# One convolution pair in every slot, begun in slot 10 of the image two ahead, with rounding 12 pairs ahead

## What is computed

```python
# layer 0: quantised 3x3 convolution
v = _gn(x)                                   # 8 groups of 2 channels, per image
scale_input = max(abs(v)) / 128              # over ALL images
x_q = round(clip(v / scale_input, -127, 127))
x = x + conv3x3(x_q, weight_int8) * (scale_input * scale_weight) + bias
# layer 1: 3x3 convolution in the frequency domain
X = rfftn(_gn(x), axes=(-2, -1))
Yr = conv(Xr, wr) - conv(Xi, wi) + b_real
Yi = conv(Xr, wi) + conv(Xi, wr) + b_imag
x = x + irfftn(Yr + 1j * Yi)
```

## Time and profile before

| what | us |
|---|---|
| median of 3 executions (lowest, highest) | 3791.02 (3787.89, 3796.55) |
| the profiled execution | 3767.42 |
| its span, first to last instruction | 3765.6 |
| first pass and set-up, to the first halo copy | 597.2 |
| statistics of slot 10 (L855), first and last of the 32 | 674.8 and 3671.6 |

### The profile page before, as it was taken

The page is one execution under the profiler, slowest core; times in us unless marked ns, Lnnn a source line. Parts: engine busy times, 40 slices in busy tenths (PEclk is TensorE's granted clock), DMA queues, the critical chain, the costliest instruction groups (busy, mean ns, idle before and its releaser), DMA issues.

```text
span 3765.6 us, 126495 instructions
## 1 busy us (share of the span) xinstructions
PE 2979.5 (79%) x45732; PEld 2646.9 (70%) x45732; DVE 3117.7 (83%) x5880; ACT 1893.1 (50%) x2799; POOL 1490.4 (40%) x1984
## 2 busy tenths in 40 slices
PE   0000004899999999999999989999999999999998
PEld 0000002788888888888888878888888888888888
DVE  8999994688878888888888878888888888888876
ACT  8999981344444444444444434444444444444443
POOL 4777000344334344343343334333433433333444
PEclk9999999999999999999999999999999999999999
DMA  8767650366666666666666656666666666666655
GB/s 309 241 236 242 236 188 16 118 196 198 198 188 196 197 195 197 194 192 195 199 194 191 195 178 194 194 192 195 192 194 191 196 192 194 193 199 191 198 179 179
DMA packets 630696, 730.98 MB, mean 194 GB/s; under 512 B 76752, under 2 KB 602160, under 8 KB 614736
## 3 DMA queue, kind: packets, MB, share of 16 engines
q1 hardware_dynamic: 482640, 588.71, 48.6%
q10 hardware_dynamic: 147456, 134.28, 12.7%
HBM read 262.58 MB, written 134.22 MB: 105 GB/s over the span
## 4 chain that ended last, share of the span: by engine, by line
PE 50%; SPq 16%; issue 11%; DMA 11%; DVE 9%; ACT 1%; POOL 1%; ACTq 1%; DVEq 0%; POOLq 0%
PE y_ps L985 12%; PE mean_b L1030 10%; SPq L454 9%; PE conv_ps L1017 7%; PE x_ps L972 6%; DMA stack<-xn 5%; PE fin_ps L1004 5%; SPq L376 4%; PE t_ps L963 3%; DMA out<-img 3%; PE conv_ps L1019 3%; DVE scaled L758 2%; DMA img<-in_x 2%; PE fin_ps L999 2%; DVE scaled L759 1%
## 5 line engine op out<-in xcount | busy, mean ns | idle before, releaser
L729 POOL TENSOR_SCALAR eo<-img,norm 128x256 f32<-128x256 f32 x512 | 481.5, 940 | 1502.1 <-PE t_ps L963 1274.2
L985 PEld LDWEIGHTS y_ps<-mix_w,stack 128*128 128x128 f16 x24576 | 787.5, 99 | 158.1 <-DMA stack<-xn 84.6
L985 PE MATMUL y_ps<-mix_w,stack 128*128 128x64 f16 x24576 | 810.4, 194 | 62.4 <-DMA stack<-xn 62.0
L540 ACT ACTIVATE xt<-t_ps 128x512 f32<-128x512 f32 x512 | 305.8, 597 | 910.8 <-PE t_ps L963 802.9
L554 ACT ACTIVATE y_hi<-y_ps 128x512 f16<-128x512 f32 x512 | 305.8, 597 | 535.4 <-PE y_ps L985 534.4
L834 DVE SCALAR_TENSOR_TENSOR img<-conv_ps,cst,img 128x512 f32<-128x512 f32 x512 | 382.3, 747 | 226.9 <-PE conv_ps L1019 226.4
L821 DVE SCALAR_TENSOR_TENSOR xn<-x_ps,norm,xn 128x512 f16<-128x512 f32 x512 | 383.1, 748 | 220.7 <-ACT xn L547 215.6
L1030 PE MATMUL mean_b<-row_mean,img 128*128 128x48 f32 x4096 | 538.2, 275 | 16.6 <-DVE img L834 16.2
L972 PE MATMUL x_ps<-dft,xt 128*128 128x128 f32 x4096 | 543.0, 276 | 0.0
L1030 PEld LDWEIGHTS mean_b<-row_mean,img 128*128 128x128 f32 x4096 | 511.3, 196 | 31.7 <-DVE img L834 31.5
L972 PEld LDWEIGHTS x_ps<-dft,xt 128*128 128x128 f32 x4096 | 499.7, 192 | 0.1
(11 more groups left out here) (134 smaller groups left out, 5138.9 us busy)
## 6 DMA issues: line engine op xcount, KB each, us to landing
stack<-xn SPq DMA_DIRECT2D x2048, 132.0 KB, 2.6
img<-in_x SPq DMA_DIRECT2D x1024, 128.0 KB, 2.8
out<-img ACTq DMA_DIRECT2D x1024, 128.0 KB, 3.0
img<-in_x SPq DMA_DIRECT2D x120, 1024.0 KB, 4.9
halo<-quant SPq DMA_DIRECT2D x192, 193.3 KB, 3.3
halo<-quant SPq DMA_DIRECT2D x64, 169.1 KB, 3.0
row_mean<-table_row_mean SPq DMA_DIRECT2D x1, 768.0 KB, 15.4
spread<-table_spread SPq DMA_DIRECT2D x1, 512.0 KB, 14.4
```

Source lines behind the costliest of these rows:

```text
L729: nc.gpsimd.tensor_scalar(even, rows[:, :, 0:F], norm[v][:, 2:3], None, ALU.add).then_inc(shift_s, 1)
L985: last = nc.tensor.matmul(y_ps[t % 2][:, g, b, :], stack[:, t % 2, g, first:first + F], mix_w[:, 2 * at + b, g, f, part, :], start=i == 0, ...
```

## The change

The table `CONV_OF` goes. Every slot t now has one convolution pair: pair t + 6 of the next image in slots 0 to 9, pair t - 10 of the image two ahead in slots 10 to 15. The row means follow one slot later, but those of pairs 0 to 5 are held until slots 14, 15 and 0, two to a slot. Rounding runs 12 pairs ahead. Loads, stores and halo copies move with it: the halo copies stand in slots 8, 12, 0 and 4 for quarters 0 to 3, a pair is stored one slot after it is finished (before: two) and loaded two slots after (before: three). The rounding ahead of the main pass is replaced by one more period with neither layer 1 nor row means in it. `halo_rows`, `conv_pair`, `row_means`, `round_pair` and `layer0_pair` themselves are unchanged.

```diff
-CONV_OF = [[j] if j < 4 else [2 * j - 4, 2 * j - 3] if j < 10 else [] for j in range(PAIRS)]
-AHEAD = 10
+AHEAD = 12
+CONV_LEAD = 6
+MEANS_OF = {14: (0, 1), 15: (2, 3), 0: (4, 5), **{t: (t + 5,) for t in range(1, 11)}}
...
+        def conv_of(t):
+            return (1, t + CONV_LEAD) if t < PAIRS - CONV_LEAD else (2, t - PAIRS + CONV_LEAD)
+        def means_of(t):
+            return (2 if t >= PAIRS - 2 else 1), MEANS_OF.get(t, ())
         def periods(engine, period):
+            period(-1, 0, False, False, True)
             period(-1, 1, False, True, True)
...  SP
-                    if mix and t >= 3 and ahead:
+                    if mix and t >= 2 and ahead:
-                        load_pair(s + 2, u, t - 3)
+                        load_pair(s + 2, u, t - 2)
-                    if later(s, mix) and t < 3 and conv:
+                    if later(s, mix) and t < 2 and conv:
-                        load_pair(s + 1, 1 - u, t + PAIRS - 3)
+                        load_pair(s + 1, 1 - u, t + PAIRS - 2)
                     if runs(mix, conv, t + 3):
                         restack(s, t + 3)
-                    if t in (2, 6) and conv:
+                    if t in (0, 4) and conv:
                         halo_rows(s + 1, t // 4 + 2)
-                    if t in (10, 14) and ahead:
+                    if t in (8, 12) and ahead:
                         halo_rows(s + 2, t // 4 - 2)
...  ACT
-                    if mix and t >= 2:
-                        store(s, u, t - 2)
-                    if later(s, mix) and t < 2:
-                        store(s - 1, 1 - u, t + PAIRS - 2)
+                    if mix and t >= 1:
+                        store(s, u, t - 1)
+                    if later(s, mix) and t == 0:
+                        store(s - 1, 1 - u, PAIRS - 1)
-            for j in range(AHEAD):
-                scale_pair(0, 0, j)
             periods(act, period)
...  DVE
-                    if pairs:
-                        layer0_pair(s + 1, 1 - u, pairs[0])
+                    d, c = conv_of(t)
+                    if conv if d == 1 else ahead:
+                        layer0_pair(s + d, (u + d) % 2, c)
                     if conv and t == STATS_AT:
                         stats_var(s + 1)
                     if conv if t < PAIRS - AHEAD else ahead:
                         d, jq = quant_of(t)
                         round_pair(...)
-                    for c in pairs[1:]:
-                        layer0_pair(s + 1, 1 - u, c)
...  PE
-                    if conv and t == STATS_AT:
-                        row_means(s + 1, 1 - u, PAIRS - 1)
-                        group_stat(s + 1, meane_s, 0, gmean_s)
                     if conv and t == IMAGE_AT:
                         centre_rows(s + 1, 1 - u)
-                    for c in pairs[:1]:
-                        if c:
-                            row_means(s + 1, 1 - u, c - 1)
-                        conv_pair(s + 1, c)
+                    d, means = means_of(t)
+                    if conv if d == 1 else ahead:
+                        for c in means:
+                            row_means(s + d, (u + d) % 2, c)
+                    if conv and t == STATS_AT:
+                        group_stat(s + 1, meane_s, 0, gmean_s)
+                    d, c = conv_of(t)
+                    if conv if d == 1 else ahead:
+                        conv_pair(s + d, c)
...
-                    for c in pairs[1:]:
-                        row_means(s + 1, 1 - u, c - 1)
-                        conv_pair(s + 1, c)
```

More of the change, by code:

```diff
@@ L459, in period @@
                 for t in range(PAIRS):
-                    if mix and t >= 3 and ahead:
-                        sp.wait_ge(store_s[(t - 3) % STORES], stored(s, t - 3))
+                    if mix and t >= 2 and ahead:
+                        sp.wait_ge(store_s[(t - 2) % STORES], stored(s, t - 2))
                         sp.sem_inc(tick_s, 1)
-                        load_pair(s + 2, u, t - 3)
-                    if later(s, mix) and t < 3 and conv:
-                        sp.wait_ge(store_s[(t - 3) % STORES], stored(s - 1, t + PAIRS - 3))
+                        load_pair(s + 2, u, t - 2)
+                    if later(s, mix) and t < 2 and conv:
+                        sp.wait_ge(store_s[(t - 2) % STORES], stored(s - 1, t + PAIRS - 2))
                         sp.sem_inc(tick_s, 1)
-                        load_pair(s + 1, 1 - u, t + PAIRS - 3)
+                        load_pair(s + 1, 1 - u, t + PAIRS - 2)
                     if runs(mix, conv, t + 3):
                         restack(s, t + 3)
-                    if t in (2, 6) and conv:
+                    if t in (0, 4) and conv:
                         halo_rows(s + 1, t // 4 + 2)
-                    if t in (10, 14) and ahead:
+                    if t in (8, 12) and ahead:
                         halo_rows(s + 2, t // 4 - 2)
@@ L485, in _ @@
                     sp.sem_inc(pair_s[u][j], 1)
-            for c in range(2):
-                halo_rows(0, c)
             periods(sp, period)
@@ L591, in period @@
                         nc.scalar.activation(im_f[:, F:N], image_ps[:, 1, :], ACT.Copy).then_inc(imf_s, 1)
-                    if mix and t >= 2:
-                        store(s, u, t - 2)
-                    if later(s, mix) and t < 2:
-                        store(s - 1, 1 - u, t + PAIRS - 2)
+                    if mix and t >= 1:
+                        store(s, u, t - 1)
+                    if later(s, mix) and t == 0:
+                        store(s - 1, 1 - u, PAIRS - 1)
             act.wait_ge(scale_s, 1)
-            for j in range(AHEAD):
-                scale_pair(0, 0, j)
             periods(act, period)
-            for t in (PAIRS - 2, PAIRS - 1):
-                store(samples - 1, 1, t)
+            store(samples - 1, 1, PAIRS - 1)
         @block.gpsimd
@@ L907, in period @@
                 for t in range(PAIRS):
-                    pairs = CONV_OF[t] if conv else []
                     if mix:
@@ L928, in period @@
                         d, jq = quant_of(t)
-                        round_pair(s + d, jq, not mix and d == 1)
-                    for c in pairs[1:]:
-                        layer0_pair(s + 1, 1 - u, c)
+                        round_pair(s + d, jq, isinstance(i, int) and s + d == 0)
                     if mix:
@@ L937, in _ @@
             dve.wait_ge(weights_1, HB + 1)
-            for j in range(AHEAD):
-                round_pair(0, j, True)
             periods(dve, period)
```

## The result

The changed kernel takes 4325.19 us (4 executions, 4320.41 to 4329.93), the kernel before, run beside it, 3789.45 us: a ratio of 1.142, 95% interval 1.138 to 1.146. Slower, as forecast and by the mechanism forecast, but by 536 us where 394 were forecast, and 15 us past the upper end of the range. The profiled execution took 4329.93 us.

What follows compares the result with a forecast made beforehand. PE's own work was taken as the bound; -2.1 - 0.9 + 12.1 + 3.6 = +12.7 us a period, x 30 + 10 = +391, gave 4158, scaled to 4185 us. The range was 4005 to 4310.

Steps and rivals of the forecast that it cites:

- The bound and the gain: Whole rhythm: PE's own work fills the two-convolution slots; shorter waits elsewhere win 2.1 and 0.9 us a period.
- stacked rows and first layer: PE's waits for stacked rows, first layer and a halo copy were to go: -2.1 us a period.
- fold and statistics together: PE's waits for POOL's folding and the statistics, 2.7 us a period, were to fall by 0.9; bounds 0 and -2.7.
- The halo copies: PE in slots 5, 1 and 13 waits 3.9, 3.7 and 4.5 us for copies: +12.1 a period, bounds 10.5 and 13.5.
- Slot 13's wait: Slot 12's copy lands at about T + 11.0, slot 13's convolution is due at T + 6.3: 4.5 us.
- The clock: Low clock behind each of three halo waits costs 1.2 us, 3.6 a period; bounds 0 and 2.4 each.
- The row of slot 10: Profile row: behind a 1.24 us statistics wait, a 4.24 us window at mean clock 0.65, read as 1.2 us lost.
- Waits longer than I have them: Rival: halo copies land in up to 5.4 us and the clock stays low twice as long: 4355 us, 7%.
- No price of the clock: Rival: same halo waits, but nothing lost to a lower clock behind them: 4075 us, 23%.
- The copy lands in time: Rival: no halo waits, all other steps standing, so the kernel gets faster: 3710 us, 6%.
- The change doesn't level anything: Rival: PE full in either layout, stack waits persist, halo waits replace them one for one: 3790 us, no change, 4%.

Runs made afterwards that it cites:

- the fastest kernel: Changed kernel with the halo copy first in SP's slot and the loads of pairs one slot later, as before the change: 3657.24 us, ratio 0.969.
- the load last: Changed kernel with the load moved behind restack and the halo copy in SP's list: 4251.58 us, ratio 1.124.
- The two load experiments: Changed kernel with the load behind restack and halo copy, 4251.58 us; changed kernel with loads alone as before the change, three slots after, 4249.84 us.
- the filled runs: Changed kernel with 28 or 14 extra matmuls in front of the convolutions of pairs 3, 7 and 11: 4182.56 us and 4268.81 us.
- the copy first: Changed kernel with the halo copy ahead of load and restack in SP's slots 0, 4, 8 and 12: 3693.45 us, ratio 0.977.

## Why the prediction was right in kind and too small

**The bound and the gain: right.** PE's own work sets the period; the stack waits went to nothing, as worked out. Slots are 5.32 us rather than 5.52. The rhythm without halo waits and without the clock (below) is 115.6 - 16.5 - 6.6 = 92.5, where 94.0 stood in the sum; the fastest kernel has 93.5 with 0.3 of halo waits left. So the change's own gain is 4.0 to 4.5 a period, not 3.0. The waits fell as forecast: 2.1 for stacked rows and first layer, and 1.0 for fold and statistics together (80.1 us to 20.4 + 16.2 + 12.6 = 49.2), where 0.9 was taken off. The rest is PE's own work, some 92.0 a period before and 90.9 after with waits and clock taken off; no run shows why.

**The halo copies, mis-sized: 12.1 a period forecast, 16.5 measured.** Kind, slots and cause were right. The term that failed is the one charged at nothing: "The load starts at T + 1.9 and is off the queue at T + 3.3, ahead of restack's T + 4.88: 0". The distance from store to load is indeed still one slot, but the slot had become 1.8 us shorter, and the time from a store's issue to the load that waited for it had not: by the timelines its median is 4.3 us before and 4.2 after. The row that I read for it came from a slot of 7.1 us, and the 170 us that SP's loads waited for stores in the kernel before were not counted at all. So in slot 4 the load starts at T + 3.8 at the earliest and at T + 4.6 in the median, and the copies of slots 0, 4 and 12 go 0.8, 1.3 and 0.8 later on average than with the load last. The prediction named the case ("if stores ran 2 us later, restack and halo would too") but left it inside its bound of 13.5.

The two load experiments give this part as 2.9 a period. The remaining 1.4 (13.5 with the load out of the way, over whole periods, against 12.1) is spread over the three waits: 4.2, 4.3 and 5.1 where 3.7, 3.9 and 4.5 stood. I had taken something off each for shorter restacks, but they take 2.7 to 2.9 on average. Slot 4's copy is in at T + 11.7, as worked out; those of slots 0 and 12 at T + 13.0 and T + 11.3, where 12.5 "at most" and 11.0 stood. Slot 13's wait was also miscounted: its own figures give 11.0 - 6.3 = 4.7, not 4.5. And the heading of that step was wrong, without harm to the sum: before the change the copies for pairs 3, 7 and 11 stood five, three and one slots ahead of them, so that pair 11 kept its one slot and lost only its late place within it.

**The clock, mis-sized: 3.6 a period forecast, about 6.6 measured.** The prediction charged each wait with the 1.2 us read behind a wait of 1.2 us, and gave 2.4 as the other end. Slot 5 takes 13.06 on average, less 5.32 of work and 5.50 of wait: 2.2; slot 1 likewise 12.40 - 5.32 - 4.92 = 2.2; slot 13 13.80 - 5.64 - 5.92 = 2.2, 5.64 being its length without a wait in the fastest kernel. Of each, 0.16 to 0.18 would stand there at full clock too, so that the clock's part is 2.0 to 2.1. The row of slot 10 was a poor stand-in, and not a typical one: in 19 of 29 periods slot 10 of the kernel before takes 6.64 with the same wait and nothing behind it is slow; in ten it takes 1.4 to 1.6 longer. Behind a halo wait of 5 us the low clock falls on the convolution and the mixing: in the rows above they lose 0.63 and 0.91. By the Trainium skill, TensorE: Matmul & The Clock Gate, Part 1 (the HAM clock gate), activity lifts the clock and idleness lowers it; the trace agrees, and the filled runs show it from the other side, by putting activity in.

**Together.** +4.4 of waits and +3.0 of clock less 1.5 of larger gain are 5.9 a period, 177 us in 30; the median lies 5 us below the profiled execution, not 0.6% above, which takes some back. That the miss is no larger is in part luck: both costs came out larger than forecast, but so did the gain, by PE's work being shorter for a reason not known. The range's upper end had 13.5 for the waits, which was too little, and 2.0 for the clock, which was about right.

**The rivals.** "Waits longer than I have them" (4355, at 7%) comes nearest to the time, 30 us above it, but not by its reason: the clock's price is nearly its 2.4, while the copies land as fast as before (median 3.2 us, longest 4.8) and are issued later instead. "No price of the clock" (4075) falls by the filled runs. "The copy lands in time" (3710) is false of the change but true of the edited kernels: 3693 with the copy moved within its slot. "The change doesn't level anything" falls by the same run.

## What to carry to other kernels

When work is levelled over slots, every hand-written distance in slots shrinks in microseconds: go through each copy, load and store and ask in microseconds, from its issue to its landing, whether it still fits, the ones whose distance in slots is unchanged too. A transfer that nobody waits for may stand ahead of one that decides; its wait is then that one's price, so order a strictly ordered queue by who is needed first, and look at what the slot before leaves on it. And charge a stall of PE with the work behind it at the lower clock, from a row in which the same kind of matmul runs at that clock.

## What the runs showed of the hardware

- A stall of PE of 5 us costs about 2.2 us more behind its end, 2.0 to 2.1 of it by the clock. Three 512-column convolution matmuls took 1.44 us instead of 0.81 and the 48 of the mixing 2.47 instead of 1.56.
- Matmuls whose result nobody uses pay for themselves here: 28 of them in each wait made the kernel 143 us faster. Removing the wait was worth 632.
- Stalls of 2.4 to 4.0 us (means of the three slots), with 14 matmuls ahead of them, still let the clock fall behind many of them (mean 0.954).
- A short stall need not lower the clock: with the copy first, 41 of 45 halo waits, up to 2.4 us long, cost 0.16 to 0.18 us beyond their length. Nor is it safe: in slot 10 of the kernel before, the clock was low behind a wait of 1.12 us in 10 of 29 periods.
- From the issue of a store's first DMA to the load that waited for it were 4.4 us in slot 4 above (2577.41 to 2581.82). The median was 4.2 in the changed kernel and 4.3 in the one before, whose slots are longer; in most cases it lay between 3.8 and 5.5.
